# A mixture-of-experts transformer layer on one core: the experts' third tile made full, the residual's products moved, the last routed sums added up beforehand

## The chip, the cores and the metric

The kernel runs on one core of one Trainium2 chip. The metric is device microseconds (us) of one launch, first to last instruction of the program and what lies around it. TensorE (PE) multiplies matrices, and its weight loads are recorded separately (PEld). ScalarE is ACT, VectorE is DVE, GpSimd is POOL, and SyncE (SP) issues most of the DMA transfers (SPq are its issues). PSUM is the memory that TensorE writes to.

## The reference

Two attentions in a row (one with a sparse or dense prior, one causal) are added to the input x, then comes a gated temporal mixer with a layer norm, and its output goes through a mixture of experts that is added to x again. B = 2, S = 1024, D = 256, so there are 2048 tokens. The change lies in the experts:

```python
E, K = 8, 2;  I_R, I_S = 4 * H, 8 * H;  H = 256
capacity = int(1.25 * T / E)                       # 320
xn = xf * rsqrt(mean(xf * xf) + eps)
probs = softmax(xn @ router_w.T);  topk_p, topk_i = top_k(probs, K)
rw = topk_p / sum(topk_p)
dispatch = order[:, :capacity]                     # the tokens of each expert, first come first served
xg = xf[dispatch]
eout = (silu(xg @ rg[e]) * (xg @ ru[e])) @ rd[e]
routed = zeros.at[dispatch].add(eout * (w * valid))
shared = (silu(x @ sg) * (x @ su)) @ sd
out = x_residual + shared + routed
```

## The kernel before

**Stages.** The program first writes a plan, a list of units such as `("gu", "s", 3, 7)`, and every engine then walks through the same list and issues its own part of each unit. So the order of the list is the order of work on every engine, and the engines wait for each other by semaphores. `ATT` is the plan of the attentions, `TAIL` (made by `tail_plan`) that of the mixer of batch 1, the routing and the experts. This case is about `TAIL`, from about 1100 us on.

**The shared expert** is computed in four chunks of 512 tokens (`CHUNKS`, `HALF`). Each chunk has 16 columns (`COLUMNS_S`) of 128 inner features. Column i is one `gu` unit (gate and up: four products of 128x128 weights with 512 tokens, L1997), after which ACT takes the silu (L1370) and DVE multiplies (L1748), and one `down` unit (four products with 256 moving columns into the accumulator `acc` in PSUM, L2009). `down` of column i stands behind `gu` of column i+1. The unit `resT` adds the residual to the accumulator: eight products of the transposed residual xT with the identity (L2024). It stands last in the chunk, behind `down` of column 15. ACT then copies the accumulator to `y` (L1377). Between the columns `shared_plan` hands out other units from a list, two steps for each column (`STEPS_PER_COLUMN`); a `PAUSE` takes a step and does nothing.

**The routing** of a batch (`route_plan`) is `logit` (PE, 32 thin products, L1963), `soft` (ACT), `pick` (DVE: top two, gains, one-hot masks and their running sum, L1688 to L1711), `pos` (PE: positions of the tokens in their expert's list, L1972 and L1973, which needs the running sum), `slots` (DVE) and `send` (POOL: 16 indirect transfers that scatter the tokens to `slots_in` in DRAM). Batch 1 is routed within the third chunk.

**The routed experts** come behind the third chunk, eight of them, each with 320 tokens (`CAP`) and eight columns (`COLUMNS_R`). A `gu` moves 320 columns four times. A `down` has three products, one for each tile of tokens, and the tokens are its stationary side: two tiles of 128 and a third of 64 (`TILES`, L2015). `fetch` of expert x+1 turns its tokens by transposes, three tiles in each of two halves (L2035), and stands behind `gu` 3 and `down` 2 of expert x. Its input `xg` is loaded by SP. At the end of expert x SP issues, in this order, the three weight loads of expert x+2 (`eload`, 1 MB each, L1049), the two stores of expert x's output (`eout`, L1066 and L1068, behind DVE's copies L1758 and L1759) and the two loads of the tokens of expert x+2 (`fetch`, L1059 and L1061).

**The last chunk** of the shared expert runs behind the experts. POOL gathers each token's two expert rows from DRAM (`gather`, two transfers for a tile of 128 tokens, L1148, into eight buffers `got`, so four tiles ahead, `AHEAD`), and DVE adds them with their gains to `y` (`combine`, two operations, L1769). The tiles 0 to 11 are combined between the last chunk's columns, two tiles a column from its fourth column on. The four tiles of the last chunk itself (12 to 15) are combined behind the chunk, once ACT has copied the accumulator to `y`. SP stores each tile (L1072).

**PSUM.** `wide0` and `wide1` take the `gu` products in turn (`SC`), `wide2` is the accumulator (`ACC`), two banks take transposes and routing products (`BT`).

Of the kernel before, what the change touches and what calls it, by code (L numbers as in the profile page):

```python
# [5 lines left out]
ALU = mybir.AluOpType  # L6
# [427 lines left out]


def route_plan(b):
    return [("logit", b), ("soft", b), ("pick", b), ("pos", b), ("slots", b), ("send", b)]


def shared_plan(tc, others):  # L440
    plan = []
    for i in range(COLUMNS_S):
        plan.append(("gu", "s", tc, i))
        if i:
            plan.append(("down", "s", tc, i - 1))
        for _ in range(STEPS_PER_COLUMN):
            if others:
                plan += flat([others.pop(0)])
    return plan + [("down", "s", tc, COLUMNS_S - 1), ("resT", tc)]


def tail_plan():
    last, route = (1, 1, NQ // 2 - 1), route_plan(0)
    others = [("num", *last), *route[:3], ("inv", *last), *route[3:5], ("times", *last), *route[5:], PAUSE]
    others += [outputs(1, 1)[k:k + NH] for k in (0, NH)] + mix_plan(1)
    plan = shared_plan(0, others) + shared_plan(1, others) + flat(others)
    plan += [("eload", 0), ("eload", 1)] + shared_plan(2, route_plan(1)) + [("fetch", 0)]
# [17 lines left out]
    mine = []  # L475
    for f in shared_plan(CHUNKS - 1, others):
        if f is None:
            continue
        mine += [("combine", f[1]), ("gather", f[2])] if f[0] == "combine" else [f]
    for f in others:  # L480
        mine += [("combine", f[1]), ("gather", f[2])]
    return plan + mine + [("combine", t) for t in range(last, B * NT)]


AHEAD = 4
# [2 lines left out]
def build(nc, A, out):  # L488

    with ExitStack() as ctx:  # L490
# [204 lines left out]
        def big_at(k, n):  # L695
            return big[:, k * S:(k + n) * S]

        act_e = big_at(12, 3)[:, 0:I_R // P * CAP].rearrange("p (i n) -> p i n", n=CAP)


        def columns_of(ap):
# [86 lines left out]
        down_done_p = signal("pe_down", [u for u in of("down") if u[1] == "s" or u[3] < COLUMNS_R - 1])  # L788
# [8 lines left out]
        done = signal("store_out", range(B * NT), 16)  # L797


        V = {ab: [u for u in of("v") if u[1:3] == ab] for ab in ((0, 0), (0, 1), (1, 0), (1, 1))}  # L800
# [50 lines left out]
            return weigh_p.after((n, u)) if to_pool(n, u) else SC.emptied(("score", n, u))  # L851

        def down_done(kind, x, i):
            return acc_done.after((kind, x)) if kind == "e" and i == COLUMNS_R - 1 else down_done_p.after(("down", kind, x, i))
# [13 lines left out]
        def _(e):  # L868
# [170 lines left out]
            for u in TAIL:  # L1039
# [10 lines left out]
                elif kind in ("num", "inv"):  # L1050
                    division(u)
                elif kind == "fetch":
                    x = u[1]
                    for b in range(B):
                        w.wait_ge(sent[b].end)
                    if x >= 2:
                        w.wait_ge(BT.filled(("xT", x - 2, DC - 1)))
                    rows = slots_in[x * CAP:(x + 1) * CAP, :]
                    e.dma_start(xg[:, x % 2, 0:2], rows[0:2 * P, :].rearrange("(t p) n -> p t n", p=P)  # L1059
                                ).then_inc(xg_in[x % 2].handle, 16)  # L1060
                    e.dma_start(xg[0:CAP - 2 * P, x % 2, 2], rows[2 * P:CAP, :]).then_inc(xg_in[x % 2].handle, 16)  # L1061
                elif kind == "eout":
                    x = u[1]
                    w.wait_ge(ACC.emptied(("acc", "e", x)))
                    rows = slots_out[x * CAP:(x + 1) * CAP, :]
                    e.dma_start(rows[0:2 * P, :].rearrange("(t p) n -> p t n", p=P), e_out[:, x % 2, 0:2]  # L1066
                                ).then_inc(eo_done[x % 2].handle, 16)
                    e.dma_start(rows[2 * P:CAP, :], e_out[0:CAP - 2 * P, x % 2, 2]).then_inc(eo_done[x % 2].handle, 16)  # L1068
                elif kind == "combine":
                    t = u[1]  # L1070
                    w.wait_ge(comb_d.after((t, TOPK - 1)))
                    e.dma_start(out[t * P:(t + 1) * P, :], y[:, t]).then_inc(done.handle, 16)  # L1072
            w.wait_ge(done.end)


        @block.gpsimd
        def _(e):
# [16 lines left out]
            for u in ATT:  # L1094
# [24 lines left out]
                elif u[0] == "score" and u[1:] in capped_p.value:  # L1119
                    first = first_of(u[1], *place(*u[1:])[0:2])  # L1120
                    p = prob_tile(u[1:])[:, :, first:first + P]
                    w.wait_ge(SC.emptied(u))
                    e.affine_select(p, p, [[0, PAIRS_OF], [1, P]], ALU.is_ge, 0.0, base=0,  # L1123
                                    channel_multiplier=-1).then_inc(capped_p.handle, 1)
            for u in TAIL:
                if u[0] == "times":
                    times(u)
                elif u[0] == "send":
                    b = u[1]
# [25 lines left out]
        def _(e):  # L1155
# [200 lines left out]
            for u in TAIL:  # L1356
# [7 lines left out]
                elif kind == "gu":  # L1364
# [6 lines left out]
                elif kind == "resT":  # L1371
                    tc = u[1]
# [17 lines left out]
        def _(e):  # L1390
# [273 lines left out]
            for u in TAIL:  # L1664
# [66 lines left out]
                elif kind == "gu":  # L1731
# [6 lines left out]
                        if SHARED[u] >= 3:  # L1738
                            w.wait_ge(down_done(*GUS_S[SHARED[u] - 3][1:]))
                    else:  # L1740
                        dst = act_e[:, i]
                        if x:
                            w.wait_ge(down_done("e", x - 1, COLUMNS_R - 1))
                        else:
# [15 lines left out]
                                  ).then_inc(ACC.empty_sem(("acc", "e", x)), 1)  # L1760
                elif kind == "combine":
                    t = u[1]
                    w.wait_ge(ACC.emptied(("acc", "s", t // TPC)))
                    for k in range(TOPK):
                        g = got_of[t, k]
                        w.wait_ge(got_in[g].after((t, k)))
                        if k:
                            w.wait_ge(comb_d.after((t, k - 1)))
                        e.scalar_tensor_tensor(out=y[:, t], in0=got[g], scalar=gain[:, k, t:t + 1], in1=y[:, t],  # L1769
                                               op0=ALU.mult, op1=ALU.add).then_inc(comb_d.handle, 1)  # L1770


        @block.tensor
        def _(e):
# [172 lines left out]
            for u in TAIL:  # L1947
# [52 lines left out]
                elif kind == "down":  # L2000
# [4 lines left out]
                    w.wait_ge(SC.emptied(("gu", of_, x, i)))  # L2005
                    if of_ == "s":
                        a = act_s[:, SHARED["gu", "s", x, i] % 3]
                        for t in range(TPC):
                            m = e.matmul(acc[:, t * D:(t + 1) * D], a[:, t * P:(t + 1) * P], wsd[i // ROWS_B][:, i % ROWS_B],  # L2009
                                         start=(i == 0 and t % 2 == 0), stop=False, skip_group_check=True)  # L2010
                        m.then_inc(down_done_p.handle, 1)
                    else:
                        wd_ = expert_w[x % 2][2]
                        for t, (o, n) in enumerate(TILES):
                            m = e.matmul(acc[0:n, t * D:(t + 1) * D], act_e[:, i, o:o + n], wd_[:, i],  # L2015
                                         start=(i == 0 and t % 2 == 0), stop=(i == COLUMNS_R - 1),
                                         skip_group_check=True)
                        m.then_inc((acc_done if i == COLUMNS_R - 1 else down_done_p).handle, 1)
                elif kind == "resT":
                    tc = u[1]  # L2020
                    acc = ACC.tile(("acc", "s", tc))
                    for t in range(TPC):
                        for c in range(DC):
                            m = e.matmul(acc[:, t * D + c * P:t * D + (c + 1) * P],  # L2024
                                         xT[:, c, tc * HALF + t * P:tc * HALF + (t + 1) * P], F["ident"], start=False,
                                         stop=True, skip_group_check=True)
                    m.then_inc(acc_done.handle, 1)
                elif kind == "fetch":
                    x = u[1]
                    w.wait_ge(xg_in[x % 2].after((x, 1)))  # L2030
                    for c in range(DC):
# [90 lines left out]
```

## Time and profile before

| | |
|---|---|
| time, median of 3 runs | 1764.71 us (1763.86 to 1764.94) |
| the profiled execution: its own time | 1770.11 us |
| its span, first to last instruction | 1768.1 us |
| mean granted TensorE clock | 0.939 |
| PE busy | 1612.8 us (91%) |
| DVE, ACT, POOL busy | 922.5 us, 737.5 us, 692.1 us |
| DMA | 121.43 MB, 69 GB/s over the span |
| instructions | 20457 |

A float32 product leaves two records on PE, each with its weight load, and a transpose leaves one; so an x8 of L1997 is one `gu` unit, and an x6 of L2015 one `down` unit of a routed expert. The starts in the trace are us from the span's start. The clock is given as a share of 2.4 GHz: 1.00 is 2.4 GHz, 0.50 is 1.2 GHz.

### The profile page before, as it was taken

To read this page: it belongs to the slowest core of one execution; us is meant where nothing else is said; L and a number is where in the kernel's file an instruction comes from. 1 tells how busy PE (TensorE), PEld (TensorE's weight loads), DVE (VectorE), ACT (ScalarE), POOL (GpSimd) and SP (SyncE) were. 2 spreads that over 40 slices of the span, in tenths; PEclk is the share of its full clock that TensorE was granted. 3 is DMA by queue.
4 is the path that set the end of the run, shared out by engine and by line. 5 is a ranking of instruction groups with operands and counts; after the bars stand their busy time and mean duration, and the time that the engine had idled before them with its cause. 6 is when DMAs were issued, how large, how long until landed. Compare 5 with 4: busy or idle time off the path is not lost.

```text
span 1768.1 us, 20457 instructions
## 1 busy us (share of the span) xinstructions
PE 1612.8 (91%) x7376; PEld 753.3 (43%) x7376; DVE 922.5 (52%) x2045; ACT 737.5 (42%) x1028; POOL 692.1 (39%) x481
## 2 busy tenths in 40 slices
PE   5789989878998998888999887999998999999998
PEld 3423322222332333333343333545665566666655
DVE  7679878789777867446764732333312111111131
ACT  4744655455565565455645566133221111111111
POOL 5437989766798997132211110300002000000060
PEclk9569999899999999988998988999999999999999
DMA  3450213133131310354232103300030004243052
GB/s 107 141 142 19 67 34 87 48 80 80 50 85 33 74 43 12 76 132 102 71 85 55 38 26 117 95 2 0 1 143 7 18 2 171 87 146 113 15 108 35
DMA packets 75905, 121.43 MB, mean 69 GB/s; under 512 B 14920, under 2 KB 53265, under 8 KB 72731
## 3 DMA queue, kind: packets, MB, share of 16 engines
q1 hardware_dynamic: 72155, 113.62, 23.0%
q0 software_dynamic: 3072, 6.03, 1.9%
q8 instruction: 58, 0.95, 0.2%
q10 hardware_dynamic: 576, 0.47, 0.1%
q14 instruction: 44, 0.36, 0.1%
HBM read 85.08 MB, written 36.96 MB: 69 GB/s over the span
## 4 chain that ended last, share of the span: by engine, by line
PE 43%; DVE 3%; ACT 2%; DMA 2%; SPq 1%; issue 1%; ACTq 0%; DVEq 0%
PE wide L1997 20%; PE wide L2009 6%; PE wide L2015 5%; PE bank L1792 3%; PE wide L1938 2%; PE wide L1918 2%; PE bank L1891 1%; DMA sb_xg<-slots_in 1%; DVE sb_rowmax L1597 1%; ACT sb_prob L1326 1%; PE bank L1784 1%; PE bank L1822 1%; PE wide L1792 1%; PE wide L1891 0%; PE bank L2035 0%
## 5 line engine op out<-in xcount | busy, mean ns | idle before, releaser
L1118 POOL TENSOR_TENSOR sb_prob<-sb_prob,sb_weight 128x1024 f32<-128x1024 f32 x192 | 450.3, 2374 | 78.9 <-ACT sb_prob L1326 78.1
L1326 ACT ACTIVATE sb_prob<-wide 128x1024 f32<-128x1024 f32 (+3 forms) x384 | 347.5, 917 | 263.7 <-PE wide L1923 146.1
L1918 PE MATMUL wide<-sb_stack_q,sb_stack_k 99*128 99x512 bf16 (+3 forms) x896 | 288.4, 371 | 25.7 <-ACT sb_prob L1326 11.6
L1891 PE MATMUL bank<-sb_stack_k,sb_stack_q 96*128 96x512 bf16 (+3 forms) x606 | 224.7, 387 | 38.8 <-DVE sb_rowmax L1597 16.2
L1370 ACT ACTIVATE sb_sil<-wide 128x320 f32<-128x320 f32 (+1 forms) x128 | 66.2, 517 | 462.6 <-PE wide L1997 462.6
L1603 DVE CUSTOM_DVE_ANT_0 sb_junk<-bank,sb_bias 128x512 bf16<-128x512 f32 x347 | 231.4, 687 | 52.8 <-PE bank L1891 50.2
L1997 PE MATMUL wide<-sb_weight,sb_ffn 128*128 128x512 f32 x512 | 235.8, 604 | 0.0
L1938 PE MATMUL wide<-sb_prob,sb_v_aug 128*17 128x512 f32 (+3 forms) x1792 | 228.1, 579 | 4.7 <-ACT sb_o_raw L1339 4.4
L1748 DVE TENSOR_TENSOR sb_act_s<-sb_sil,wide 128x512 f32<-128x512 f32 x64 | 44.0, 687 | 271.4 <-ACT sb_sil L1370 271.4
L1597 DVE TENSOR_REDUCE sb_rowmax<-bank 128x1 f32<-128x512 f32 (+3 forms) x259 | 136.7, 552 | 76.2 <-PE bank L1894 57.4
L1148 POOL DMA_INDIRECT sb_weight<-slots_out,sb_slot_r x32 | 31.4, 982 | 319.7 <-issue 311.6
L1123 POOL TENSOR_SCALAR_AFFINE_SELECT sb_prob<-sb_prob 128x256 f32<-128x256 f32 x128 | 52.3, 416 | 262.2 <-ACT sb_prob L1326 261.5
L1997 PE MATMUL wide<-sb_xgT,sb_big 128*128 128x320 f32 x512 | 152.7, 444 | 1.1 <-ACT sb_xgT L1385 1.1
L1891 PEld LDWEIGHTS bank<-sb_stack_k,sb_stack_q 96*128 96x128 bf16 x606 | 60.1, 100 | 215.3 <-issue 83.0
L1923 PE MATMUL wide<-sb_unlisted,sb_cut 128*128 128x512 bf16 x384 | 149.3, 389 | 0.0
L1997 PEld LDWEIGHTS wide<-sb_weight,sb_ffn 128*128 128x128 f32 x512 | 98.3, 194 | 101.7 <-issue 99.3
L1918 PEld LDWEIGHTS wide<-sb_stack_q,sb_stack_k 99*128 99x128 bf16 x896 | 82.9, 101 | 126.4 <-issue 29.4
L1748 DVE TENSOR_TENSOR sb_big<-sb_sil,wide 128x320 f32<-128x320 f32 x64 | 31.2, 488 | 201.6 <-ACT sb_sil L1370 201.6
L1891 PE MATMUL wide<-sb_stack_k,sb_stack_q 96*128 96x512 bf16 (+3 forms) x290 | 112.6, 388 | 14.9 <-DVE sb_rowmax L1597 6.8
L1603 DVE CUSTOM_DVE_ANT_0 sb_junk<-wide,sb_bias 128x512 bf16<-128x512 f32 x165 | 113.3, 687 | 24.6 <-PE wide L1891 23.0
L2009 PE MATMUL wide<-sb_ffn,sb_act_s 128*128 128x256 f32 x512 | 120.5, 379 | 0.0
L1135 POOL DMA_INDIRECT slots_in<-sb_bias,sb_slot_w x32 | 32.7, 1020 | 213.0 <-DVE sb_slot_r L1730 203.7
(257 smaller groups left out, 1952.7 us busy)
## 6 DMA issues: line engine op xcount, KB each, us to landing
sb_stack_k<-parts SPq DMA_DIRECT2D x32, 256.0 KB, 6.9
o_raw<-sb_o_raw SPq DMA_DIRECT2D x32, 256.0 KB, 2.3
sb_big<-rg SPq DMA_DIRECT2D x8, 1024.0 KB, 5.0
sb_big<-ru SPq DMA_DIRECT2D x8, 1024.0 KB, 7.2
sb_big<-rd SPq DMA_DIRECT2D x8, 1024.0 KB, 10.5
sb_stack_q<-parts SPq DMA_DIRECT2D x16, 384.0 KB, 5.1
parts<-sb_o_norm SPq DMA_DIRECT2D x48, 128.0 KB
sb_stack_q<-parts SPq DMA_DIRECT2D x16, 256.0 KB, 5.5
```

What stands on the lines that cost most here:

```text
L1118: e.tensor_tensor(p, p, weight_of(*u[1:]), ALU.mult).then_inc(weigh_p.handle, 1)
L1326: e.activation(p[:, :, first:HALF], sc[:, :, first:HALF], ACT.Exp).then_inc(SC.empty_sem(u), 1)
L1597: e.tensor_reduce(acc, BK.tile(u)[:, 0:hi - lo], AX.X, ALU.max).then_inc(BK.empty_sem(u), 1)
L1603: e.tensor_tensor_reduce(out=junk[:, i % 2, 0:hi - lo], in0=BK.tile(u)[:, 0:hi - lo], in1=bias[:, qt, lo:hi], scale=1.0, scalar=-3e38, op0 ...
L1748: e.tensor_tensor(dst, sil[:, j % 2, 0:n], gu[:, HALF:HALF + n], ALU.mult).then_inc(SC.empty_sem(u), 1)
L1891: i = e.matmul(bk[:, 0:hi - lo], stack_q[0:ROWS, n % 3, h, qt * P:(qt + 1) * P], stack_k[0:ROWS, n % 3, h, lo:hi], start=True, stop=not diag)
L1918: i = e.matmul(sc[:, j * HALF + first:(j + 1) * HALF], stack_k[0:ROWS_M, n % 3, g, kt * P:(kt + 1) * P], stack_q[0:ROWS_M, n % 3, g, half ...
L1923: i = e.matmul(sc[:, j * HALF:(j + 1) * HALF], cut[:, JOBS[n][1]], unlisted[:, kt, half * HALF:(half + 1) * HALF], start=False, stop=True)
L1938: i = e.matmul(pv_bank[g * HB:g * HB + DH + 1, first:HALF], v_aug[:, kt, q * QUAD + g, :], prob_tile((n, v))[:, j, first:HALF], start=kt = ...
L1997: m = e.matmul(gu[:, o:o + n], wt[:, c, col * P:(col + 1) * P], src[c], start=(c == 0), stop=(c == DC - 1))
L2009: m = e.matmul(acc[:, t * D:(t + 1) * D], a[:, t * P:(t + 1) * P], wsd[i // ROWS_B][:, i % ROWS_B], start=(i == 0 and t % 2 == 0), stop=Fa ...
L2015: m = e.matmul(acc[0:n, t * D:(t + 1) * D], act_e[:, i, o:o + n], wd_[:, i], start=(i == 0 and t % 2 == 0), stop=(i == COLUMNS_R - 1), ski ...
```

## The change

The edit has these parts.

1. The third tile of the routed experts has 128 rows in place of 64 (`ROOM` = 384 places a column in place of 320). The rows behind the 64 are zeroed once, by two memsets on POOL: in `xg` when the attentions are done, in `act_e` when the mixer is done. Both `fetch` and `down` use full tiles. What is loaded, what is stored and what `gu` computes stay at 320.
2. `resT` stands ahead of the chunk's last `down` unit, in all four chunks. The signal that the accumulator is complete moves to the last `down`.
3. The route of batch 1 has four pauses (two columns) between `pick` and `pos`.
4. The combines of the last four tiles are handed out between the columns like the others (the first operation of such a tile writes gain times row to `y` in place of adding to it), and the whole stream begins at the third column in place of the fourth. Behind the chunk a new unit `total` adds the accumulator to `y`, two tiles at a time, on DVE, and SP stores two tiles behind each. ACT copies the accumulator in the first three chunks alone.

```diff
-TILES = [(0, P), (P, P), (2 * P, CAP - 2 * P)]
+TILES = 3
+ROOM = TILES * P
 def route_plan(b):
-    return [("logit", b), ("soft", b), ("pick", b), ("pos", b), ("slots", b), ("send", b)]
+    return [("logit", b), ("soft", b), ("pick", b)] + [PAUSE] * (4 * b) + [("pos", b), ("slots", b), ("send", b)]
 def shared_plan(tc, others):
-    return plan + [("down", "s", tc, COLUMNS_S - 1), ("resT", tc)]
+    return plan + [("resT", tc), ("down", "s", tc, COLUMNS_S - 1)]
 def tail_plan():
-    others = [None] * 6
-    for t in range(last):
-        others += [("combine", t, t + AHEAD)]
...
-    return plan + mine + [("combine", t) for t in range(last, B * NT)]
+    others = [PAUSE] * 4
+    for t in range(B * NT):
+        others += [[("combine", t), ("gather", t + AHEAD)] if t + AHEAD < B * NT else ("combine", t)]
+    plan += shared_plan(CHUNKS - 1, others) + flat(others)
+    return plan + [("total", t) for t in range(last, B * NT, 2)]
# SP
+                elif kind == "total":
+                    w.wait_ge(total_d.after(u))
+                    for t in range(u[1], u[1] + 2):
+                        e.dma_start(out[t * P:(t + 1) * P, :], y[:, t]).then_inc(done.handle, 16)
# POOL
+            e.memset(xg[CAP - 2 * P:P, :, TILES - 1], 0.0).then_inc(padded.handle, 1)
...
+                    e.memset(act_e[:, :, CAP:ROOM], 0.0).then_inc(padded.handle, 1)
# DVE
+                        if last and not k:
+                            e.tensor_scalar(y[:, t], got[g], gain[:, k, t:t + 1], None, ALU.mult).then_inc(comb_d.handle, 1)
...
+                elif kind == "total":
+                    t, k = u[1], u[1] % TPC
+                    acc = ACC.tile(("acc", "s", CHUNKS - 1))
+                    w.wait_ge(comb_d.after((t + 1, TOPK - 1)))
+                    w.wait_ge(acc_done.after(("s", CHUNKS - 1)))
+                    e.tensor_tensor(y[:, t:t + 2], acc[:, k * D:(k + 2) * D].rearrange("p (t n) -> p t n", t=2),
+                                    y[:, t:t + 2], ALU.add).then_inc(total_d.handle, 1)
# PE, down of a routed expert
-                        for t, (o, n) in enumerate(TILES):
-                            m = e.matmul(acc[0:n, t * D:(t + 1) * D], act_e[:, i, o:o + n], wd_[:, i],
+                        w.wait_ge(padded.end)
+                        for t in range(TILES):
+                            m = e.matmul(acc[:, t * D:(t + 1) * D], act_e[:, i, t * P:(t + 1) * P], wd_[:, i],
# PE, fetch
-                        for t, (o, n) in enumerate(TILES):
-                            m = e.transpose(BT.tile(key_)[:, o:o + n], xg[0:n, x % 2, t, c * P:(c + 1) * P],
-                                            F["ident"][0:n, 0:n])
+                        for t in range(TILES):
+                            m = e.transpose(BT.tile(key_)[:, t * P:(t + 1) * P], xg[:, x % 2, t, c * P:(c + 1) * P], F["ident"])
```

## Rows read from the trace of the kernel before

**Rows 1.** Busy us (count) of PE, PEld, DVE, ACT, POOL; clock, DMA share, GB/s.

```profile
1425.00:1676.00 251.00, 250.69 (x938) 157.58 (x938) 38.29 (x78) 34.12 (x78) 0.00 (x0) 1.00 0.26 93
```

**Rows 2.** Chain that ended last, expert 1 (start us, us, what).

```profile
1456.63 4.50 PE wide L1997 x16
1461.13 1.44 PE wide L2015 x6
1462.57 2.35 PE wide L1997 x8
...
1470.15 1.15 PE bank L2035 x6
...
1485.02 3.09 PE wide L2015 x12
```

**Rows 3.** The same chain, the last chunk's last two down units and resT.

```profile
1755.38 3.47 PE wide L2009 x16
1758.85 1.80 PE wide L2024 x16
```

**Rows 4.** Groups by shape from 1100 us on: busy us, mean ns, idle before.

```profile
L2009 PEld LDWEIGHTS wide<-sb_ffn,sb_act_s 128*128 128x128 f32 x512 | 97.0, 190 | 39.1 <-issue 28.7 <-DVE sb_act_s L1748 0.5
L2015 PEld LDWEIGHTS wide<-sb_big 128*64 128x64 f32 x128 | 12.2, 134 | 21.2 <-issue 21.2
L1748 DVE TENSOR_TENSOR sb_act_s<-sb_sil,wide 128x512 f32<-128x512 f32 x64 | 44.0, 687 | 271.4 <-ACT sb_sil L1370 271.4
L1831 PE MATMUL bank<-sb_const_f,sb_bias 128*128 128x128 f32 x16 | 2.2, 272 | 0.0
```

**Rows 5.** SP's issues at the end of expert 1.

```profile
1488.12 0.37 SPq L1049 DMA_DIRECT2D sb_big<-rg  x1
...
1493.88 0.59 SPq L1061 DMA_DIRECT2D sb_xg<-slots_in  x1
```

**Rows 6.** The chain again: the landing of the second of these loads.

```profile
1493.88 7.78 DMA sb_xg<-slots_in
```

**Rows 7.** SP's issues at the end of expert 4.

```profile
1582.85 0.37 SPq L1049 DMA_DIRECT2D sb_big<-rg  x1
...
1588.40 0.48 SPq L1061 DMA_DIRECT2D sb_xg<-slots_in  x1
```

**Rows 8.** DMA issues from 1575 to 1607 us: KB, us to landing.

```profile
sb_xg<-slots_in SPq DMA_DIRECT2D x1, 64.0 KB, 6.7
```

**Rows 9.** PE's timeline at expert 0's first gu, and the busy time (as group 1) behind it.

```profile
1425.12 4.55 PE L1997 MATMUL wide<-sb_xgT,sb_big 128*128 128x320 f32 x16 [1.06 <-ACT sb_xgT L1385]
...
1425.20:1436.00 10.80, 10.80 (x40) 7.06 (x41) 1.46 (x3) 1.31 (x3) 0.00 (x0) 1.00 0.01 2
```

**Rows 10.** Timeline of PE at pos of batch 1; brackets: idle before, releaser.

```profile
1343.91 0.19 PE L1972 MATMUL bank<-sb_before,sb_const_bf 128*128 128x8 bf16 x1 [4.42 <-DVE sb_before L1711]
```

**Rows 11.** The chain behind it: its gu unit, and a later one.

```profile
1344.51 6.23 PE wide L1997 x8
...
1352.46 3.43 PE wide L1997 x8
```

**Rows 12.** Busy time by stretch, as group 1: that gu unit.

```profile
1344.40:1350.70 6.30, 6.30 (x13) 2.72 (x11) 0.00 (x0) 0.00 (x0) 0.00 (x0) 0.57 0.01 3
```

**Rows 13.** Timeline of the kernel's end.

```profile
1760.67 1.21 ACT L1377 ACTIVATE sb_bias<-wide 128x256 f32<-128x256 f32 x4 [4.66 <-PE wide L2024]
1761.92 4.03 DVE L1769 SCALAR_TENSOR_TENSOR sb_bias<-sb_weight,sb_gain,sb_bias 128x256 f32<-128x256 f32 x8 [5.12 <-ACT sb_bias L1377]
```

**Rows 14.** DMA issues from 1765.9 us on: the last store.

```profile
out<-sb_bias SPq DMA_DIRECT2D x1, 128.0 KB, 1.7
```

**Rows 15.** Timeline of POOL: the fourth gather; brackets: idle before, releaser.

```profile
1684.81 0.95 POOL L1148 DMA_INDIRECT sb_weight<-slots_out,sb_slot_r  x1 [0.31 <-issue]
```

**Rows 16.** DMA issues from 1722.75 us on: a late gather's landing.

```profile
sb_weight<-slots_out,sb_slot_r POOLq DMA_INDIRECT x1, 9.0
```

**Rows 17.** Timeline of DVE: the first combines.

```profile
1694.80 2.05 DVE L1769 SCALAR_TENSOR_TENSOR sb_bias<-sb_weight,sb_gain,sb_bias 128x256 f32<-128x256 f32 x4
```

More of the change, by code:

```diff
@@ L471, in tail_plan @@
     plan += [("gather", t) for t in range(AHEAD)]
-    others = [None] * 6
-    for t in range(last):
-        others += [("combine", t, t + AHEAD)]
[L475 to L481, printed above, removed]
-    return plan + mine + [("combine", t) for t in range(last, B * NT)]
+    others = [PAUSE] * 4
[3 more added lines that the diff above has]
+    return plan + [("total", t) for t in range(last, B * NT, 2)]
 AHEAD = 4
@@ L787, in build @@
         silu_a = signal("act_silu", of("gu"))
-        down_done_p = signal("pe_down", [u for u in of("down") if u[1] == "s" or u[3] < COLUMNS_R - 1])
+        down_done_p = signal("pe_down", [u for u in of("down") if u[3] < (COLUMNS_S if u[1] == "s" else COLUMNS_R) - 1])
         acc_done = signal("pe_acc", [u[1:3] for u in of("down") if u[3] == 0])
@@ L796, in build @@
         comb_d = signal("dve_comb", [(u[1], k) for u in of("combine") for k in range(TOPK)])
-        done = signal("store_out", range(B * NT), 16)
+        total_d = signal("dve_total", of("total"))
+        padded = signal("pool_pad", ["rows", "columns"])
+        OUT_TILES = [u[1] for u in of("combine") if u[1] < B * NT - TPC] + [u[1] + k for u in of("total") for k in range(2)]
+        done = signal("store_out", OUT_TILES, 16)
         V = {ab: [u for u in of("v") if u[1:3] == ab] for ab in ((0, 0), (0, 1), (1, 0), (1, 1))}
@@ L853, in down_done @@
         def down_done(kind, x, i):
-            return acc_done.after((kind, x)) if kind == "e" and i == COLUMNS_R - 1 else down_done_p.after(("down", kind, x, i))
+            final = (COLUMNS_S if kind == "s" else COLUMNS_R) - 1
+            return acc_done.after((kind, x)) if i == final else down_done_p.after(("down", kind, x, i))
         attention_done = [BK.emptied(u) for u in banked[-BANKS:]] + [PV.emptied((len(JOBS) - 1, NH - 1))]
@@ L1068, in _ @@
                     e.dma_start(rows[2 * P:CAP, :], e_out[0:CAP - 2 * P, x % 2, 2]).then_inc(eo_done[x % 2].handle, 16)
-                elif kind == "combine":
+                elif kind == "combine" and u[1] in OUT_TILES[0:-TPC]:
                     t = u[1]
@@ L1124, in _ @@
                                     channel_multiplier=-1).then_inc(capped_p.handle, 1)
+            for mark in attention_done:
+                w.wait_ge(mark)
+            e.memset(xg[CAP - 2 * P:P, :, TILES - 1], 0.0).then_inc(padded.handle, 1)
+            w.wait_ge(padded.after("rows"))
             for u in TAIL:
-                if u[0] == "times":
+                if u == ("eload", 0):
+                    for mark in mixer_done:
+                        w.wait_ge(mark)
+                    e.memset(act_e[:, :, CAP:ROOM], 0.0).then_inc(padded.handle, 1)
+                elif u[0] == "times":
                     times(u)
@@ L1370, in _ @@
                     e.activation(sil[:, i % 2, 0:n], SC.tile(u)[:, 0:n], ACT.Silu).then_inc(silu_a.handle, 1)
-                elif kind == "resT":
-                    tc = u[1]
+                elif kind == "down" and u[1] == "s" and u[3] == COLUMNS_S - 1 and u[2] + 1 < CHUNKS:
+                    tc = u[2]
                     acc = ACC.tile(("acc", "s", tc))
@@ L1762, in _ @@
                     t = u[1]
-                    w.wait_ge(ACC.emptied(("acc", "s", t // TPC)))
+                    last = t >= B * NT - TPC
+                    if last:
+                        w.wait_ge(sent[B - 1].end)
+                    else:
+                        w.wait_ge(ACC.emptied(("acc", "s", t // TPC)))
                     for k in range(TOPK):
@@ L1768, in _ @@
                             w.wait_ge(comb_d.after((t, k - 1)))
-                        e.scalar_tensor_tensor(out=y[:, t], in0=got[g], scalar=gain[:, k, t:t + 1], in1=y[:, t],
-                                               op0=ALU.mult, op1=ALU.add).then_inc(comb_d.handle, 1)
+                        if last and not k:
+                            e.tensor_scalar(y[:, t], got[g], gain[:, k, t:t + 1], None, ALU.mult).then_inc(comb_d.handle, 1)
+                        else:
+                            e.scalar_tensor_tensor(out=y[:, t], in0=got[g], scalar=gain[:, k, t:t + 1], in1=y[:, t],
+                                                   op0=ALU.mult, op1=ALU.add).then_inc(comb_d.handle, 1)
+                elif kind == "total":
[5 more added lines that the diff above has]
+                                    y[:, t:t + 2], ALU.add).then_inc(total_d.handle, 1)
         @block.tensor
@@ L2007, in _ @@
                         a = act_s[:, SHARED["gu", "s", x, i] % 3]
+                        final = i == COLUMNS_S - 1
                         for t in range(TPC):
                             m = e.matmul(acc[:, t * D:(t + 1) * D], a[:, t * P:(t + 1) * P], wsd[i // ROWS_B][:, i % ROWS_B],
-                                         start=(i == 0 and t % 2 == 0), stop=False, skip_group_check=True)
-                        m.then_inc(down_done_p.handle, 1)
+                                         start=(i == 0 and t % 2 == 0), stop=final, skip_group_check=True)
+                        m.then_inc((acc_done if final else down_done_p).handle, 1)
                     else:
                         wd_ = expert_w[x % 2][2]
-                        for t, (o, n) in enumerate(TILES):
-                            m = e.matmul(acc[0:n, t * D:(t + 1) * D], act_e[:, i, o:o + n], wd_[:, i],
+                        w.wait_ge(padded.end)
+                        for t in range(TILES):
+                            m = e.matmul(acc[:, t * D:(t + 1) * D], act_e[:, i, t * P:(t + 1) * P], wd_[:, i],
                                          start=(i == 0 and t % 2 == 0), stop=(i == COLUMNS_R - 1),
@@ L2030, in _ @@
                     w.wait_ge(xg_in[x % 2].after((x, 1)))
+                    w.wait_ge(padded.after("rows"))
                     for c in range(DC):
```

7 lines of the change are left out of this document (3 added, 4 removed).

## The prediction

> **What bounds the kernel now.** I read the page first, for shares, then busy time by stretch. In the stretch that the change touches most, the routed experts, TensorE is busy for all but 0.3 of 251 us at the full clock of 2.4 GHz, while DVE and ACT are busy for 15% of it at most [rows 1]. The reader is to see that only two things can gain there: fewer or shorter intervals on PE, and less behind its last product. The chain that ended last was read next, because there each unit is one interval; it runs over PE's units one behind another [rows 2, 3]. Then the groups by shape, to see which product costs more than its like [rows 4], SP's issues with their landings, to see what a faster PE would run into [rows 5 to 8], and the timelines at `pos`, at the end and at the gathers [rows 10, 13, 15, 17].
>
> **The third tile.** A record of 256 moving columns takes 3.47/16 = 0.217 us where all tiles are full [rows 3], so six should take 1.30. A routed `down` takes 1.44. Two of them back to back take 3.09, so the second costs 1.65, of which 0.21 is neither its own nor the first one's [rows 2]. Likewise two `gu` units back to back take 4.50, but one alone behind a `down` takes 2.35: so the second of the pair costs 2.15, and whichever unit comes first behind a third tile pays 0.20 [rows 2]. A 64-wide third tile thus costs 0.14 on the way in and 0.20 on the way out. The loads say why: those of 64 columns stand behind 21.2 us of idle time marked as issue, 0.33 for each of the 64 tiles: such a load is not pulled ahead under the running product but waits for its end [rows 4]. With 128 columns in all tiles I expect none of that, since the moving side (256 columns) is what the 0.217 us is for. An expert is 8 `gu`, 8 `down` and a `fetch`: 1485.02 + 3.09 - 1456.63 = 31.48 us, 30.33 without the `fetch` of 1.15 [rows 2]. Afterwards 8 x 2.15 + 8 x 1.30 = 27.60. Saved 2.73 each, 21.8 in all. Bounds: 20 to 22.5, from rounding and the two ways to split a pair.
>
> The Trainium skill speaks against this edit in one place and understates it in another. "TensorE: Matmul & The Clock Gate" (Step-by-step, LDWEIGHTS) has the load's time scale with its column count; the trace agrees, with 134 ns for 64 and 190 ns for 128 columns [rows 4]. Were these 56 ns exposed for each of the 128 records, the edit would give back 7.2 us and save 14.6; but in the shared chunks loads of 190 ns fit under intervals of 217 ns [rows 3, 4]. "TensorEngine Tiling (Array Packing)" (Key Properties) says that a change of tiling mode drains the engine. If the first page's drain of about 128 cycles were all of it, my estimate would be 0.05 us a switch, two switches a tile, 7 us in all; the rows show 0.34 a tile, and I go by them.
>
> **The transposes** get 64 more columns in two of six, and lose four switches. A full transpose takes 2.2/16 = 0.14 [rows 4], so six take 0.83 where they took 1.15 [rows 2]: 0.32 saved in seven fetches (that of expert 0 is followed by a wait for ACT anyway [rows 9]), 2.2 in all. Bounds: 0, if a transpose behind `down` costs more than in that row, to 2.5.
>
> **What comes late next: the tokens' load.** PE will reach the `fetch` earlier. It stands behind four `gu` and three `down` units: today 4.50 + 3 x 1.44 + 2 x 2.35 = 13.52 us after the expert's start, afterwards 4 x 2.15 + 3 x 1.30 = 12.50 [rows 2]. The load it needs does not hang on PE's pace. SP issues it behind three weight loads and two output stores, which start at the end of the expert before, at 1488.11; the second piece lands at 1493.88 + 7.78 = 1501.66, or 13.55 after [rows 5, 6]. Today that is just in time: the margin is -0.03. Six fetches have such a load; four land 13.3 to 13.6 us after the start, two 12.3 to 12.6, as the one issued at 1588.40, 5.6 after its start at 1582.8, and landed in 6.7 [rows 7, 8]. Against 12.50 PE waits 0.8, 1.05, 0.8, 1.1, 0 and 0.05 us, 3.8 in all given back. Bounds: 0 (another landing) to 6.5 (all six like the worst). A wait of some 1 us does not lower the clock in this trace: behind the one of 1.06 us at expert 0 it stays at 1.00 [rows 9].
>
> **`pos` two columns later.** PE waits 4.42 us there for DVE's running sum, and behind it PE is granted 0.57 in the mean (mostly 1.2 GHz), so that one `gu` takes 6.23 in place of 3.43 [rows 10 to 12]. Two columns are 10.3 us (one is 3.43 + 1.73 [rows 3, 11]), more than twice the wait, and the units put in front (`gu` 2 and 3, `down` 1 and 2) need results that DVE has by then: `down` 2 comes some 8 us behind the place of `pos` today, and DVE is free after 4.4. Saved 4.42 + 2.80 = 7.2. `slots` and `send` start about 6 us later; the 16 scatters then end some 45 us ahead of the first `fetch`. Bounds: 4.4, if the clock falls without the wait too, to 7.2.
>
> **`resT` ahead of the last `down`** costs nothing and brings nothing: the two last `down` units already run 3.47 us for 16 records, with no gap [rows 3]. What it could cover, the multiply of column 15, is hidden behind `down` 14. PE's work is the same, so the last product ends where it did. The three ACT copies that stay have the same distance to PE's next use. The memsets on POOL, the few waits on `padded`, and the eight combines that move lie on engines that wait for PE meanwhile [rows 1]; without that cover they would be about 1, 0 and 4 us.
>
> **The end.** Today 0.02 us behind the last product ACT starts, copies for 1.21, DVE adds for 4.03 up to 1765.95, and the span ends at 1768.1: 7.45 us behind PE's last product at 1758.85 + 1.80 = 1760.65 [rows 3, 13]. Afterwards two DVE additions of 128x512 out of PSUM, 0.69 each [rows 4], so 0.7 to the first and 1.35 to the second. SP issues two stores behind each; one issue is 0.37 to 0.59 [rows 5, 7], so the last goes out near 2.1, lands 1.7 later [rows 14], and 0.45 is left to the span's end as today (1765.97 + 1.7 to 1768.1): 4.3. Saved 3.1; bounds 2.5 to 3.6.
>
> **The gathers** are what the earlier stream leans on. The first two tiles are combined 5.16 us earlier, at 1689.7 [rows 17]; their fourth gather is issued at 1684.81 [rows 15] and its kind lands in under 3 us, so there is no wait. Later ones land in up to 9.0 [rows 16], and an odd tile's second gather will have 6.3 us, so DVE waits up to some 2.7 us in the last two combining columns. PE sees this only past 6.2 us (2.5 of DVE's own idle time a column, and 3.7 until `down` needs the product). Price: 0.
>
> **Sum.** -21.8 - 2.2 + 3.8 - 7.2 - 3.1 = -30.5 us. The profiled execution has 1770.11, so 1739.6; the median of the runs lies 5.4 below it, so 1734.2, taken as 1734.
>
> **Rivals.**
> - A, as worked out, 1734, own range 1731 to 1738: 0.64.
> - B, the tokens' load lands with the faster pace, or ahead of it as in two of six: no 3.8, 1730.5: 0.10. Against it: its order on SP is unchanged, and four of six were late.
> - C, the full third tile pays its longer load: the gain shrinks by 7.2, 1741.5: 0.07. Against it: the intervals of [rows 3].
> - D, `pos` is free of its wait, but the clock falls all the same, because the thin `logit` products lie shortly before: 2.8 less, 1737: 0.10.
> - F, the new waits of 1 us lower the clock as the one of 4.42 did, each with 2.8 us behind it [rows 11]: four times, 11.2, 1745.5: 0.05. Against it: [rows 9].
> - G, the other side: gathers starve DVE, and DVE starves PE. The eight combining columns would each have to grow by 30.5/8 = 3.8 us, thus a gather take (5.16 + 3.8)/4 = 2.24 us where POOL issues one in 1.26 (0.95 and 0.31 before it [rows 15]). Below 1.3 us it costs nothing; at 2.3 the kernel is slower, 1766: 0.02. Against it: no combine waited so far, with 7 us between issue and use; for it, the landing time that grew to 9.0 [rows 16].
>
> What is left, 0.02, are cases that I do not see. The range 1729 to 1742 takes in B, D, C and the bounds of the unknown terms. A measurement of this kernel tells 0.2% (3.5 us) from no change. Faster by more than that holds in all cases but G and part of the rest: 0.97; within it 0.01; slower 0.02.
>
> **What would show it.** A `gu` unit in the experts' stretch at 2.15, a `down` at 1.30, a `fetch` near 0.83, one expert at 28.5 to 29.5 us; PE waiting on the load of `xg` about 1 us in four experts; no PE idle time in front of L1972 in batch 1, and 3.43 for the `gu` behind it; 4.3 us from the last product to the end. Wrong would be a `down` still above 1.4 (C), `gu` units above 3 us behind the `xg` waits (F), or PE waiting for L1748 in the last chunk (G).

## The result, and the profile after

| | before | after |
|---|---|---|
| median in the first comparison | 1764.83 us (4 runs) | 1738.64 us (4 runs) |
| ratio, 95% interval | | 0.9849 (0.9826 to 0.9871) |
| median in a second comparison | 1769.05 us (9 runs) | 1735.49 us (5 runs) |
| ratio, 95% interval | | 0.9816 (0.9787 to 0.9844) |
| span of the profiled execution | 1768.1 us | 1736.6 us |
| PE busy | 1612.8 us (91%) | 1582.0 us (91%) |

The change makes the kernel 1.5% to 1.8% faster, 26 or 34 us by the medians. The forecast was 1734, with 1729 to 1742 as its range; 1738.6 lies in it.

The medians are blurred by something that the change doesn't touch. Cut by PE's first product of each stage (in us; "again" is a second profile of the same kernel; the last column is what lies behind PE's last product), the profiles read:

| profile | to first logit | to logit of batch 1 | to expert 0 | experts | last chunk | end |
|---|---|---|---|---|---|---|
| before | 1101.5 | 229.1 | 94.5 | 250.9 | 84.6 | 7.4 |
| before, again | 1106.0 | 225.8 | 94.3 | 250.6 | 84.6 | 7.4 |
| after | 1102.3 | 225.8 | 87.2 | 230.8 | 86.2 | 4.3 |
| after, again | 1101.9 | 225.8 | 87.2 | 230.8 | 84.5 | 4.3 |

From expert 0 on, the stages of one kernel agree within some 0.3 us, but for one last chunk. The attentions in front take 1094.6 to 1106.0 us over all twelve profiles of this study. The mean granted clock there is 0.92 in the shortest and 0.91 in the longest, so the clock may have a part in it; no run separates it from what else there is. So a gain is read from its stage, and the medians only confirm the sum. Second profile against second profile the last four stages give 7.1 + 19.8 + 0.1 + 3.1 = 30.1 us; in the first pair, with 1.6 us lost in the last chunk, 29.0.

Expert 0 from its `fetch` on, and expert 1 up to its own, in the chain that ended last of the changed kernel. It answers to [rows 2] (start us, us, what):

```profile
1428.01 0.66 PE bank L2062 x6
...
1430.82 1.29 PE wide L2042 x6
1432.12 2.15 PE wide L2022 x8
...
1441.17 2.63 PE wide L2042 x12
...
1445.25 2.49 SPq L1065
...
1450.22 7.12 DMA sb_xg<-slots_in
1457.39 0.88 PE bank L2062 x6
```

A `gu` (L2022) takes 2.15 or 2.16 where one behind a narrow tile took 2.35, a `down` (L2042) 1.29 for 1.44, two of them 2.63 for 3.09, a `fetch` (L2062) 0.66 for 1.15. Then, in expert 1, the chain leaves PE: it goes over SP's issues to the load of `xg`, and the `fetch` behind that landing takes 0.88. That is the new wait. The waits of PE from 1050 us on, longest in total first (us in all, times, the longest). The ones left out belong to the attentions' end and stand in the kernel before too, but for one of 0.2:

```profile
...
PE bank L2062 <- DMA sb_xg<-slots_in: 3.8, 4, 1.1
...
PE wide L2035 <- DVE sb_act_s L1759: 1.4, 1, 1.4
PE wide L2022 <- ACT sb_xgT L1396: 1.4, 1, 1.4
```

The 4.42 us in front of `pos` [rows 10] are gone (the 0.2 us that are left of such waits are batch 0's), and the `gu` behind it, which answers to [rows 11], takes 3.54 (forecast was 3.43):

```profile
1347.68 3.54 PE wide L2022 x8
```

Of the new waits, the load of `xg` costs 3.8 in four waits, 1.1 the longest. New and not foreseen at that place is the wait for L1759, the multiply of the shared chunk (L1748 in the kernel before). ACT's timeline in the last chunk shows where it comes from:

```profile
1663.45 0.60 ACT L1381 ACTIVATE sb_sil<-wide 128x512 f32<-128x512 f32 x1 [4.56 <-issue]
1673.70 1.09 ACT L1381 ACTIVATE sb_sil<-wide 128x512 f32<-128x512 f32 x2 [9.65 <-remote]
```

The silu of a column comes each 5.16 us; the one due at 1668.6 began at 1673.7, with its input ready for 5 us, and two were then done together. The end, which answers to [rows 13]:

```profile
1732.28 1.29 DVE L1794 TENSOR_TENSOR sb_bias<-wide,sb_bias 128x512 f32<-128x512 f32 x2 [3.85 <-PE wide L2035]
1733.00 1.78 SPq L1075 DMA_DIRECT2D out<-sb_bias  x4
```

Two additions in 1.29 us, four issues in 1.78, and the span ends at 1736.6, 4.3 behind PE's last product.

### The profile page after: what moved, and what is told of

It reads as the page before. It is cut to its first block, busy times and chain, and to the rows that moved or that the text cites. A ratio compares the mean times of both kernels' runs of the same rounds, so it can differ in the third digit from the quotient of the medians.

```text
span 1736.6 us, 20457 instructions
## 1 busy us (share of the span) xinstructions
PE 1582.0 (91%) x7376; PEld 766.9 (44%) x7376; DVE 921.5 (53%) x2047; ACT 735.9 (42%) x1024; POOL 692.2 (40%) x483
## 4 chain that ended last, share of the span: by engine, by line
PE 38%; DMA 4%; SPq 3%; ACT 3%; DVE 2%; issue 1%; another core or an unknown queue 1%; POOL 0%; DVEq 0%; ACTq 0%; POOLq 0%
PE wide L2022 17%; PE wide L2035 6%; PE wide L2042 3%; PE bank L1817 3%; DMA sb_xg<-slots_in 3%; PE wide L1963 2%; PE wide L1943 1%; SPq L1065 1%; ACT sb_prob L1337 1%; PE bank L1916 1%; PE bank L1847 1%; PE bank L1809 1%; DVE sb_rowmax L1608 1%; PE wide L1817 1%
## 5 line engine op out<-in xcount | busy, mean ns | idle before, releaser
L2022 PE MATMUL wide<-sb_weight,sb_ffn 128*128 128x512 f32 x512 | 230.6, 593 | 0.0
L1759 DVE TENSOR_TENSOR sb_act_s<-sb_sil,wide 128x512 f32<-128x512 f32 x64 | 44.0, 687 | 252.8 <-ACT sb_sil L1381 236.4
L2022 PE MATMUL wide<-sb_xgT,sb_big 128*128 128x320 f32 x512 | 147.1, 432 | 1.4 <-ACT sb_xgT L1396 1.4
L2022 PEld LDWEIGHTS wide<-sb_weight,sb_ffn 128*128 128x128 f32 x512 | 96.6, 190 | 98.3 <-issue 95.7
L1759 DVE TENSOR_TENSOR sb_big<-sb_sil,wide 128x320 f32<-128x320 f32 x64 | 31.2, 488 | 185.3 <-ACT sb_sil L1381 185.3
L2035 PEld LDWEIGHTS wide<-sb_ffn,sb_act_s 128*128 128x128 f32 x512 | 96.9, 190 | 40.4 <-issue 28.2
```

Source lines behind the costliest of these rows:

```text
L1759: e.tensor_tensor(dst, sil[:, j % 2, 0:n], gu[:, HALF:HALF + n], ALU.mult).then_inc(SC.empty_sem(u), 1)
L2022: m = e.matmul(gu[:, o:o + n], wt[:, c, col * P:(col + 1) * P], src[c], start=(c == 0), stop=(c == DC - 1))
```

## The experiments

**The kernel before, profiled again.** No edit.

> The kernel before, unchanged, for a second profile. The changed kernel's own units came out as forecast (experts 20.0 us shorter, end 3.1 shorter, pos 7.3 shorter), yet the medians differ by 26.2 us only, not by the spans' 31.5. Theory: the profiled execution of before had two falls of the clock that its other executions lack, behind logit of batch 0 (2.5 us) and behind the pos wait (2.8 us). Then this profile has a span of about 1763 and one or both of the two gu units at 3.43 us in place of 6.0 and 6.2, the pos wait still 4.4 us. Rival: both falls are always there, and the executions differ in the attentions, ahead of 1100 us.

Span 1768.7 us, its one time 1770.73. The wait at `pos` is 4.4 again and the clock falls behind it again: that `gu` takes 6.09 in PE's timeline, where one at full clock shows 3.60 to 3.68. (The chain, which cuts off what overlaps, has 5.95 for it, for the 6.23 of the first profile.) The fall behind the first logit is absent, and the `gu` there takes 3.68 (6.18 in the first profile).

```profile
1345.55 6.09 PE L1997 MATMUL wide<-sb_weight,sb_ffn 128*128 128x512 f32 x8
```

The theory was half right: the fall at batch 0 comes and goes, the one behind the 4.4 us wait was there in both. But the attentions took 4.5 us longer, so in part the rival holds: the scatter lies mostly in them. It also shows in the many runs of the kernel before that stand beside these experiments: 1760.56 to 1774.01 us.

**The pauses alone.**

```diff
-    return [("logit", b), ("soft", b), ("pick", b), ("pos", b), ("slots", b), ("send", b)]
+    return [("logit", b), ("soft", b), ("pick", b)] + [PAUSE] * (4 * b) + [("pos", b), ("slots", b), ("send", b)]
```

> Before with the four pauses alone. Theory (the clock falls behind the wait in few executions): 4.4 us off the median, 1760.4. Rival (the clock falls each time): 7.2 off, 1757.6. Both: no PE wait in front of pos of batch 1.

1761.27 us against 1767.85, ratio 0.9962 (0.9947 to 0.9978). That is 6.6 us by the medians, 4 to 9 by the interval, too wide to tell the theory (4.4) from the rival (7.2). No wait is left in front of `pos` of batch 1. From the logit of batch 1 to expert 0 it takes 88.9 us, between the 94.3 of before and the 87.2 of the changed kernel. The stages tell more. Where the 1.7 us above 87.2 come from is in this profile's busy time by stretch (PE, PEld, DVE, ACT, POOL; clock, DMA share, GB/s):

```profile
1332.00:1336.00 4.00, 4.00 (x7) 1.61 (x6) 0.00 (x0) 1.44 (x2) 0.00 (x0) 0.57 0.00 0
1336.00:1350.00 14.00, 14.00 (x61) 8.58 (x60) 6.20 (x43) 1.79 (x3) 0.00 (x0) 1.00 0.00 1
```

Here the clock falls right behind the 32 thin logit products, with PE busy all the time and no wait near, and `gu` 1 shows 5.38 where one at 2.4 GHz shows 3.60. So the clock can fall at this place without the wait, in some executions. That the logit products bring it down is argued from where it falls; no run took them away. In the twelve profiles of this study it happened behind batch 1's logit three times, and each of the three has a like fall of 3.4 us behind batch 0's logit, so that some 227.4 us lie between the two logits and not 225.8. The two others (the full tile alone, the narrow product twice) keep the wait, and there the clock fell a second time behind it: from logit to expert 0 they take 94.9 and 95.0 us.

**The full tile alone**, part 1 of the edit, on the kernel before.

> Before with the full third tile alone. Theory: 21.8 from 64 down units, some 3 from the fetches, less 3.8 for the waits on the tokens' load: 20 to 21 us off the median, 1744.5. Rival (the gain of the changed kernel came partly from elsewhere, and the padding is worth only what a short drain would be, or what is left once a longer load is paid): 7 to 13 off, 1752 to 1758.

1742.14 us against 1767.85, ratio 0.9865 (0.9843 to 0.9887), which is 24 us (20 to 28). The experts take 230.8 us, for 250.6 to 250.9: 19.8 to 20.1, where the prediction's terms give 20.2. The stages behind them and the end are those of before. PE waits for the load of `xg` as in the full change:

```profile
PE bank L2047 <- DMA sb_xg<-slots_in: 3.9, 4, 1.1
```

**The narrow product twice.**

```diff
                                          start=(i == 0 and t % 2 == 0), stop=(i == COLUMNS_R - 1),
                                          skip_group_check=True)
+                        m = e.matmul(acc[0:n, t * D:(t + 1) * D], act_e[:, i, o:o + n], wd_[:, i],
+                                     start=False, stop=(i == COLUMNS_R - 1), skip_group_check=True)
```

> The kernel before with the product of the 64-row third tile issued twice in a row; the rows of that tile come out doubled, all else is as before. Theory (what a narrow tile costs is the change of shape, 0.14 on the way in and 0.20 on the way out, whatever stands between): each second product adds its bare 2 x 0.217 us, 64 of them 27.8 us, so the experts take 278.6. Rival (the narrow product itself is slow, 0.77 for its two records): 64 x 0.77 = 49, so they take 300.

The added product stands behind the loop over the tiles, so it repeats the last of them. 1795.4 us against 1769.05, ratio 1.0155 (1.0123 to 1.0188). The experts take 278.2 us, 27.3 to 27.6 more than before, where the theory has 27.8 and the rival 49. The chain shows each of the doubled products (L2018) at its bare 0.43, and the intervals around it unchanged, with the slow `gu` still behind it:

```profile
1462.84 1.44 PE wide L2015 x6
1464.28 0.43 PE wide L2018 x2
1464.71 2.35 PE wide L1997 x8
```

So the narrow product is not slow. What costs is the step from one shape to the other, and it is paid once for a run of narrow products. PEld's timeline shows the same for the loads:

```profile
1463.63 0.19 PEld L2015 LDWEIGHTS wide<-sb_big 128*64 128x64 f32 x2 [0.33 <-issue]
1463.90 0.35 PEld L2018 LDWEIGHTS wide<-sb_big 128*64 128x64 f32 x2
1464.64 0.30 PEld L1997 LDWEIGHTS wide<-sb_xgT,sb_big 128*128 128x128 f32 x2 [0.38 <-issue]
```

A 64-wide load behind a full tile stands behind 0.33 us of idle time, one behind another 64-wide tile behind less than 0.1, and the first full one behind them again behind 0.38. So it is the change of shape that keeps a load from being pulled ahead, in both directions, and not the width that the prediction named.

**The end alone**, parts 2 and 4.

> Before with the residual's products moved, the combine stream begun at the third column and the last routed sums added up beforehand, tiles and route as before. Theory: 3.1 us off the end, 1761.7, and no PE wait in the last chunk. Rival (the earlier stream holds DVE or ACT up, as the 1.4 us PE wait on the multiply at 1673.7 in the changed kernel's profile suggests): 1.7 off, 1763.1, with such a wait in this profile too.

1761.22 us against 1767.85, ratio 0.9974 (0.9954 to 0.9994). The end takes 4.3 us for 7.4, the last chunk 84.6 as before, and PE does not wait in it. So neither the residual's move nor the earlier stream costs or brings anything in PE's time. That is the theory; of the rival's wait on the multiply there is nothing in this profile.

**The changed kernel again.** No edit.

> The changed kernel unchanged. So far the stages behind the first logit take the same time in every profile of one kernel, while the attentions ahead of it take between 1094.6 and 1106.0 us. Theory: the shift of the median is the sum of the stages, 28.7 us, blurred by the attentions; with more runs it lies between 26 and 30. The last chunk takes 84.6 us here, because the ACT silu that began 5 us late in the first profile was a chance event. Rival: ACT is late in each execution of this kernel, the last chunk takes 86.2 again, and that is a price of the change.

1735.49 us against 1769.05. The last chunk takes 84.5, and ACT is on time. The late silu of the first profile is thus no fixed price of the change. The median's shift, 33.6, lies above the expected 26 to 30. The two kernels' runs lie over 11.5 and 6.5 us, and the interval of the ratio (28 to 38 us) holds the 30.1 of the stages.

**The stream a column later.**

```diff
-    others = [PAUSE] * 4
+    others = [PAUSE] * 6
```

> The changed kernel with the stream of combines begun at the fourth column again. Theory (the earlier stream is no cause of the late silu): the last chunk takes 84.6 us or 86.2 as the unchanged kernel does in the run beside this one, the end 4.3, no difference in the median. Rival (gathers and stores pressed together hold ACT or DVE up): 1.5 us faster than the changed kernel, with a last chunk of 84.6 where that one has 86.2.

1736.43 us against 1735.49 of the changed kernel; last chunk 84.5, end 4.3. No difference.

**The stream from the first column.**

```diff
-    others = [PAUSE] * 4
+    others = [PAUSE] * 0
```

> The changed kernel with the stream of combines begun in the last chunk's first column. Theory (DVE waits for gathers cost nothing until they exceed what its own idle time and PE's distance to the multiply cover; the fourth gather lands about 8.5 us after the third column's begin less 10.3, thus some 12 us after the chunk's start, while the multiply behind it is needed at 12.0): PE now waits for L1759 in the first columns, 1 to 6 us in all, last chunk 85.5 to 91. Rival (the gathers are covered even so): last chunk 84.5.

The last chunk takes 90.6 us, 6.1 more than the 84.5, at the upper end of the expectation, and the kernel 1743.33, against 1767.01 of the kernel before. The waits of PE, and then DVE's timeline, in which each combine now stands behind its gather and the multiply (L1759) behind them:

```profile
PE wide L2035 <- DVE sb_act_s L1759: 4.3, 6, 1.3
```

```profile
1650.83 0.48 DVE L1787 SCALAR_TENSOR_TENSOR sb_bias<-sb_weight,sb_gain,sb_bias 128x256 f32<-128x256 f32 x1 [2.91 <-DMA sb_weight<-slots_out,sb_slot_r]
...
1654.78 0.48 DVE L1787 SCALAR_TENSOR_TENSOR sb_bias<-sb_weight,sb_gain,sb_bias 128x256 f32<-128x256 f32 x1 [0.96 <-DMA sb_weight<-slots_out,sb_slot_r]
1655.18 0.68 DVE L1759 TENSOR_TENSOR sb_act_s<-sb_sil,wide 128x512 f32<-128x512 f32 x1
```

The six waits are 4.3 us, and the chunk lost 6.1: a `down` that starts behind a wait also gives up the overlap with the product before it (0.16 in PE's timeline), and takes 1.99 there for 1.89. That is some 0.3 us a wait on top of the wait itself.

**The tokens' load ahead.** SP issues the load for expert x+2 before it waits for the end of expert x, thus behind the stores of the boundary before, a whole expert earlier than in the changed kernel. (`tokens(x)` issues the two loads.)

```diff
                     else:
+                        tokens(x)
                         w.wait_ge(down_done("e", x - 2, COLUMNS_R - 1))
...
-                elif kind == "fetch":
-                    x = u[1]
-                    for b in range(B):
-                        w.wait_ge(sent[b].end)
...
+                elif kind == "fetch" and u[1] < 2:
+                    tokens(u[1])
```

> The changed kernel, with the load of an expert's tokens issued by SP ahead of the weight loads that are issued at the same boundary, not behind them. Theory (PE waits for it 3.8 us in all because it queues behind 3 MB of weights and two stores): those waits vanish, the experts take 227 us in place of 230.8, 3.8 off the median. Rival (the weights or the output store then come late, or the DMA engines are simply full): the waits move to the weights, or the experts stay at 230 or more.

1730.61 us against 1735.49 of the changed kernel, and 1769.05 of the kernel before: ratio 0.9783 (0.9757 to 0.9809). The experts take 225.5 us, 5.2 less than 230.8, more than the 3.8 that were waited. The `fetch` says where the rest is. It takes 0.66 here, for 0.88 behind each of the six late landings:

```profile
1459.30 0.66 PE bank L2065 x6
```

The reason given in the expectation, the queue in front of the load, is not what this run shows. Issued a whole expert ahead, the second piece still lands 6.9 to 7.5 us behind its issue (the five loads behind a boundary; 2.7 for the one that has none in front), as in the changed kernel with its 6.7 to 7.9. The load is not faster, it is early enough. Whether the 3 MB of weights in front of it make it slow, no run separates.

No wait took its place. One PE wait is left in the experts' stretch:

```profile
PE wide L2025 <- ACT sb_xgT L1399: 1.4, 1, 1.4
```

**And expert 0's transposes earlier**, on top of that.

```diff
-    plan += [("eload", 0), ("eload", 1)] + shared_plan(2, route_plan(1)) + [("fetch", 0)]
+    third = shared_plan(2, route_plan(1))
+    plan += [("eload", 0), ("eload", 1)] + third[:-2] + [("fetch", 0)] + third[-2:]
```

> The kernel with the tokens' loads ahead of the weights, and in addition the transposes of expert 0 ahead of the third chunk's residual products, where the residual and the last down cover ACT's copies of them. Theory (PE's one wait for ACT at the start of the experts, 1.4 us, is all that is to be had there): from the first logit of batch 1 to the first expert's gu 86.5 us or less of what was 87.2 less the 1.4 (85.8), experts 225.5 as before, last chunk 84.5, end 4.3. Rival (ACT's copies of the tokens, which now stand ahead of its copies of the accumulator, hold back the first expert's down, or the clock): no gain.

From the logit of batch 1 to expert 0 it now takes 85.6 us for 87.2, and the wait for ACT is gone; experts, last chunk and end stay at 225.5, 84.5 and 4.3. The span is 1729.6, the shortest of all profiles. The median, 1730.77 against 1767.01 (ratio 0.9791, 0.9762 to 0.9821), cannot tell it from the kernel without this edit.

## Why the prediction was right

**The third tile: right in mechanism and size.** Forecast were 2.15 for a `gu`, 1.30 for a `down`, 27.60 an expert without its `fetch`. Measured: 2.15 or 2.16, 1.29, and (225.5 - 7 x 0.66)/8 = 27.6 in the kernel without late loads. The doubled product showed that the 0.34 a tile belongs to the change of shape. The Trainium skill's "TensorEngine Tiling (Array Packing)" (Key Properties) says that a change of tiling mode drains the engine. The trace agrees in that the price hangs on the change and not on the product; that it is a drain, no run shows. The two changes cost 0.34 us, three times the 0.1 us of the prediction's estimate, which took the drain of about 128 cycles from the Trainium skill's "TensorE: Matmul & The Clock Gate" (Step-by-step). The longer load that the Trainium skill's "TensorE: Matmul & The Clock Gate" (Step-by-step) has for more columns is there and free: 190 ns under intervals of 2.63/12 = 0.219 us. Rival C is out.

**The transposes: gain undersized.** 0.14 for a full transpose is the busy time of [rows 4] divided by 16. But these 16 stand in groups of four and eight; inside a group they start 0.11 us apart, and the busy time has the tail of each group's last record, which overlaps the product behind it. In the changed kernel six take 0.66, so 0.11 each, and a `fetch` gains 0.49 in place of 0.32: 3.4 us in all for 2.2.

**The late load: right in place, price undersized.** Forecast were waits of 0.8, 1.05, 0.8, 1.1, 0 and 0.05 us, 3.8 in all. PE waited 3.8 in four fetches. But a `fetch` that begins behind a wait takes 0.88 for 0.66, and six did, so 1.3 us came on top. (In a running stream the load of its first transpose begins 0.21 us ahead of the transpose, and the second transpose follows 0.11 behind the first; behind a wait load and transpose begin together, and the second follows after 0.17.) In all 5.2 measured by taking the load away, for 3.8. Against the sum the transposes bring 1.2 more and the late load costs 1.4 more, so that the two errors cancel to 0.2; that part of the agreement is luck. Rival B was not to be had by chance, but by moving the load. The clock did not fall at these waits: the changed kernel's profile has 1.00 over the whole stretch. Rival F is out.

```profile
1415.30:1646.20 230.90, 226.98 (x939) 173.55 (x940) 38.34 (x78) 33.39 (x78) 0.00 (x0) 1.00 0.29 101
```

**`pos`: right, with the clock's part less sure than it was taken.** 7.1 to 7.3 us against the two profiles of before, forecast 7.2. The clock fell behind the wait in all five profiles that keep it, for 6.8 us in three and for 3.4 us in two. The prediction's 45 us from the last scatter to the first `fetch` is that of the kernel before; in the changed one the scatters' tokens are loaded from 1376.9 on, 36 us ahead of that `fetch`, still far from PE. Rival D, the clock falling all the same because of the logit, is real in some executions and costs 1.7 us there (88.9 against 87.2).

**The residual's move: right, nothing.** Last chunk 84.6 with it and without.

**The end: right.** 7.4 to 4.3, 3.1 as forecast.

**The gathers: right at the column chosen.** The doubt was whether DVE's waits reach PE. They don't from the third or the fourth column on: in the second profile of the changed kernel DVE waits for gathers 6.3 us in all, 1.4 the longest, and PE never for DVE's multiply. From the first column they cost 6.1 us. Rival G needs a start two columns earlier, and then costs a fifth of what would turn the sign. What the prediction had as 0 and one profile has as 1.6 is the late silu.

**The sum** was 30.5 us; the stages give 30.1. All nine executions of the changed kernel, 1733.5 to 1741.4 us, lie in the range. The distance of the first median from the forecast, 4.6 us, is within what the attentions alone vary. The step of the working that was weak is the last one: one execution's distance to a median of three, 5.4 us, was carried over as if it belonged to the kernel, while a second profile of before was as long as the first (1768.7) for other reasons.

**Open.** What held ACT for 5 us in one of the five profiles with this stream of combines (the changed kernel twice, the end alone, and the two kernels with the earlier loads). Its input was there and no semaphore in the trace explains it. No run here settles it.

## What to carry to other kernels

A narrow tile among full ones is not cheaper in a stream of products: look for the same instruction with two durations, depending on what stands before it, and price the step in and out; zero padding to the full shape can be free, as here, where the load of the wider tile fits under the product before it. When PE gets faster by design, list every transfer whose start is tied to PE's boundary and compare its landing with PE's new arrival; a margin of 0.03 us in the old profile is the warning. And measure such edits by the stage they touch when the rest of the kernel varies by more than the edit brings.

## What the runs showed of the hardware that was not expected

- Six transposes take 0.66 us in a running stream and 0.87 or 0.88 behind a wait of 0 to 1.1 us: a restart costs some 0.2 us beyond the wait itself, and some 0.3 us at a `down` (6.1 us lost for 4.3 us of waits in six).
- The two steps between a 128-wide and a 64-wide stationary side cost 0.14 and 0.20 us, however many narrow products stand between (one or two tried). The load behind such a step stands behind 0.33 or 0.38 us of idle time, a 64-wide load behind another 64-wide one behind less than 0.1.
- Behind 32 thin products (8 moving columns each, 3.5 us) the clock fell to 1.2 GHz with PE busy all the time, in 3 of 12 profiles for batch 1 and in 4 of 12 for batch 0; two profiles of one kernel differ in it.
- The same attentions take 1094.6 to 1106.0 us from one execution to the next, while the experts and the last chunk, 315 to 335 us in one kernel or the other, repeat within some 0.4 us where ACT is on time.
